# Order of background work in a two-layer attention kernel: queries before keys for one chunk, more background calls in steps with many row maxima, and a shorter lead of the maxima

## The reference, cut to what matters

```
layer 0:  x0, x1 = halves of x (1024 rows each)
          x0 += gate * attention(ln(x0) modulated)      # each half on itself
          x1 += gate * attention(ln(x1) modulated)
          x0 attends to keys/values of x1, and x1 to those of x0 (cross)
          x += gate * mlp(ln(x) modulated)              # gelu, 256 -> 1024 -> 256
layer 1:  x = ln(x + attention(x, x, x, masked))        # 512 valid keys
          x = ln(x + attention(x, context, context))    # 1601 keys
          x = ln(x + mlp(x))                            # relu
```

## Time and profile before

| | |
|---|---|
| runs, us | 2201.14, 2204.52, 2205.17 (median 2204.52) |
| profiled execution, its own time | 2205.17 us |
| its span | 2203.3 us |
| TensorE busy | 1991.3 us, 90% of the span |
| VectorE busy | 1539.9 us, 70% |
| ScalarE busy | 1293.3 us, 59% |
| GpSimd busy | 565.4 us, 26% |
| mean granted share of TensorE's clock | 0.945 |

### The profile page before, as it was taken

One profiled execution on the slowest core, in us unless ns is written; L12 is line 12 of the kernel. 1 busy time (PEld: TensorE's weight loads), 2 busy tenths in 40 slices (PEclk: granted clock), 3 DMA queues, 4 the chain that ended last, 5 costly groups with the idle time before them and its releaser, 6 DMA issues. The chain is left out here.

```text
span 2203.3 us, 33892 instructions
## 1 busy us (share of the span) xinstructions
PE 1991.3 (90%) x12890; PEld 769.1 (35%) x12890; DVE 1539.9 (70%) x2841; ACT 1293.3 (59%) x2406; POOL 565.4 (26%) x537
## 2 busy tenths in 40 slices
PE   5898998998979899998999988999899999999976
PEld 3333222332323343533533432332253334334315
DVE  5777797797857658476376557896847996896704
ACT  1155585566746676764775653678335874684670
POOL 1135775751123211032022332210204001102100
PEclk8699999999989999999999997999799999999988
DMA  6733423422243202035024422200211020000000
GB/s 155 154 86 87 128 83 83 106 59 49 64 89 77 62 6 55 20 73 121 4 62 102 92 61 73 59 21 14 42 40 37 4 50 3 14 17 4 13 16 12
DMA packets 97338, 126.67 MB, mean 57 GB/s; under 512 B 25325, under 2 KB 82014, under 8 KB 92046
## 3 DMA queue, kind: packets, MB, share of 16 engines
q1 hardware_dynamic: 94862, 123.89, 23.7%
q10 hardware_dynamic: 2304, 0.53, 0.1%
HBM read 89.95 MB, written 24.74 MB: 52 GB/s over the span
## 5 line engine op out<-in xcount | busy, mean ns | idle before, releaser
L1691 ACT ACTIVATE PT<-ps 128x512 f32<-128x512 f32 (+1 forms) x2112 | 1109.0, 601 | 700.1 <-PE ps L1476 696.2
L1774 DVE TENSOR_REDUCE mx<-ps 128x1 f32<-128x512 f32 x2048 | 1283.7, 681 | 263.8 <-PE ps L1497 261.1
L1497 PE MATMUL ps<-KS,QS 49*128 49x512 bf16 x2048 | 744.2, 399 | 124.1 <-DVE mx L1774 63.5
L1476 PE MATMUL ps<-QS,KS 51*128 51x512 bf16 (+3 forms) x4224 | 816.7, 388 | 11.3 <-DMA QS<-mr 11.0
L1523 PE MATMUL ps<-PT,Vt 128*32 128x512 f32 (+1 forms) x4224 | 584.3, 626 | 0.0
L1497 PEld LDWEIGHTS ps<-KS,QS 49*128 49x128 bf16 x2048 | 188.0, 95 | 734.1 <-DVE mx L1774 454.8
L1476 PEld LDWEIGHTS ps<-QS,KS 51*128 51x128 bf16 (+3 forms) x4224 | 235.8, 96 | 238.6 <-ACT PT L1691 64.8
L2008 POOL CAST nm<-nm 128x16 bf16<-128x16 f32 x64 | 12.7, 198 | 513.2 <-DVE nm L1787 513.1
L1523 PEld LDWEIGHTS ps<-PT,Vt 128*32 128x32 f32 (+1 forms) x4224 | 84.2, 109 | 150.2 <-issue 147.5
L1618 PE MATMUL ps<-XT,big 128*128 128x256 f32 x512 | 126.7, 398 | 3.5 <-ACT big L1747 2.6
L1630 PE MATMUL ps<-big 128*128 128x256 f32 x512 | 114.8, 382 | 1.6 <-DVE big L1909 1.6
(11 more groups left out here) (110 smaller groups left out, 1100.8 us busy)
## 6 DMA issues: line engine op xcount, KB each, us to landing
scr<-S SPq DMA_DIRECT2D x27, 768.0 KB, 3.7
big<-in_mask_1x1xSxS_ik SPq DMA_DIRECT2D x16, 1024.0 KB, 5.2
QS<-scr SPq DMA_DIRECT2D x32, 384.0 KB, 9.6
KS<-scr SPq DMA_DIRECT2D x24, 384.0 KB, 8.7
QS<-scr SPq DMA_DIRECT2D x32, 256.0 KB, 6.1
ON<-Oe SPq DMA_DIRECT2D x256, 32.0 KB, 1.9
OD<-scr_r SPq DMA_DIRECT2D x32, 256.0 KB
KS<-scr SPq DMA_DIRECT2D x24, 256.0 KB, 4.8
```

The source lines that it names most:

```text
L1476: z = eng.matmul(ps[0:w, it.bank[1 - j], :], KS[lo:hi, part, pr, col:col + w], QS[lo:hi, part, u.qs, pr, :], start=part == 0, stop=part == ...
L1497: return eng.matmul(mbank(it)[:, 0:w], QS[lo:lo + MR, 0, u.qs, pr, 128 * it.tq:128 * it.tq + 128], KS[lo:lo + MR, 0, pr, it.lo:it.hi], sta ...
L1691: eng.activation(PT[0:w, it.pt * 4 + 2 * it.pp + 1 - k, :], ps[0:w, it.bank[k], :], ACT.Exp, scale=0.25).then_inc(S["exp_done"], 1)
L1774: eng.tensor_reduce(out=mx[:, u.b, c, it.i:it.i + 1], in_=mbank(it)[:, 0:it.hi - it.lo], axis=AX.X, op=ALU.max).then_inc(S["max_done"], 1)
```

## The change

Three edits: `LEAD` goes from 9 to 7; in a step with more than two tasks of maxima, `bg_step` is called after each task but the last; and in `kv_l0` the query projection comes ahead of the key projection and V.

```diff
-LEAD = 9
+LEAD = 7
@@
                     for task in now_[:-1]:
                         for g in task:
                             g()
+                        if len(now_) > 2:
+                            bg_step()
@@
-            return (ln_mod(c, g) + k_steps(512 * c, 512, f"k_in{c}", over, 4 * g) + v_steps(4 * c, 512, c, over)
-                    + (q_steps(c, slot, 4 * g) if slot is not None else []))
+            return (ln_mod(c, g) + (q_steps(c, slot, 4 * g) if slot is not None else [])
+                    + k_steps(512 * c, 512, f"k_in{c}", over, 4 * g) + v_steps(4 * c, 512, c, over))
```

## The result

The changed kernel took 2220.97 us (median of 4 runs, 2220.02 to 2223.06), the kernel before 2204.23 us (2201.14 to 2205.17). The ratio is 1.0072, 95% interval 1.0052 to 1.0092: slower by 0.7%, where I had forecast 2190 us and faster. The profiled execution has a span of 2218.1 us against 2203.3.

What follows compares the result with a forecast made beforehand. TensorE and VectorE were taken as both full in plain steps. Queries -11.1, calls -5.0 and -1.0, LEAD +2.5 sum to -14.6 us from 2205.17, so 2190.6, forecast as 2190 us; 8 in 10 for 2178 to 2206.

Steps and rivals of the forecast that it cites:

- an MLP at half clock: Second heavy stretch: two thirds of the moved MLP pieces run at half clock, +18 us, about 2213 us; chance 0.12.
- The third rival: Gains and losses cancel: queries edit brings only 7, stretches nothing, maxima rows cost 11, less 1.5; about 2207 us; chance 0.15.
- What bounds the kernel: Plain steps: TensorE and VectorE both full; time won only at TensorE waits, half clock, or where only one is full.
- my 3.1: Chunk 3's projection: TensorE stands still while the second eviction into `xn` waits for GpSimd, +3.1 us.
- -2.3 us of half clock: Chunk 3, 643.10 to 648.40: the half-clock stretch behind the queries' old wait goes, -2.3 us.
- -5.0 us for the second stretch: Second heavy stretch: extra calls bring the MLP inside; overlap, pace and clock gains less VectorE work sum to -5.0 us.
- the last ten slots at the plain pace: Second heavy stretch: last ten slots, behind dense TensorE work, run at 1.25 rather than 1.4 us a pair, -1.5 us.
- I had -1 us: First heavy stretch: its only background comes four steps earlier, nothing else is eligible; -1 us, between -4 and +3.
- I take +4, a third of the way: LEAD edit: later delivery of maxima rows costs +4 us in crowded places, from a range of 0 to 12.
- waits appeared in the 1601-key passes: Sign against the prediction: `QS<-mr` waits there; it expected 11 to 20 us in all, all before 900 us.
- the +12: LEAD edit: upper end of the late-delivery cost by the DMA rule alone, putting the kernel at about 2199 us.
- The -1.5 us at the end: Kernel's end: 2 of 35 steps without maxima get them, filling TensorE's room; -1.5 us, between -3 and 0.

## Why the prediction was wrong, point by point

**The number.** I forecast 2190 us and had 8 in 10 for 2178 to 2206; it is 2221, 30 us more. By the runs, some 22 of these are LEAD (24 us beside the other edits, I had +2.5), 7 the queries ahead of keys (-4.2, I had -11.1), and the calls little more than 1. Slower had a chance of 0.12, but by another mechanism, an MLP at half clock, which did not come. The third rival had the right mechanism, with 11 us for the maxima rows; its sum is 2207.7.

**What bounds the kernel.** Held. The work at full clock was the same before and after (1898.7 and 1898.6 us), and time moved only with waits and clock.

**Queries ahead of keys: right in kind, too large.** The wait near 643 is gone and the one for `xn` is there, 3.87 us against my 3.1 (ScalarE was idle for 5.88 before its eviction, where I had 3 to 4). Timeline of the kernel after:

```profile
635.42 2.12 POOL L2038 TENSOR_TENSOR S<-xn,S 128x1024 bf16<-128x1024 f32 x1
637.57 0.37 SPq L1288 DMA_DIRECT2D scr<-S  x1
637.64 0.69 ACT L1731 ACTIVATE xn<-ps,colb 128x512 f32<-128x512 f32 x1 [5.88 <-POOL S L2038]
...
638.38 3.78 PE L1584 MATMUL ps<-XT,wA 128*128 128x512 f32 x4 [3.87 <-ACT xn L1731]
```

I had priced the new wait at full clock. The four matmuls behind it took 3.78 us where the same work took 1.98: a half-clock stretch comes with this wait as it had come with the old one, 6.2 us behind it against the 5.3 of the earlier trace rows.

```profile
638.38:644.57 6.19, 6.19 (x18) 1.65 (x18) 2.04 (x3) 2.01 (x4) 1.42 (x2) 0.50 0.76 210
```

So the term "-2.3 us of half clock" did not hold. The edit brought 6.7 us in the profile and 4.2 by its ratio, not 11.1.

**Extra calls: right in sign.** I had -5.0 us for the second stretch, with bounds of 19 both ways. The traces show -8.6 and -5.1, the ratio of the run with the calls alone -4.6 for the whole kernel. The MLP ran inside, at 0.38 us for output pieces, so the rival with the MLP at half clock fell. Windows of the kernel after, the stretch and what follows (the two together answer to the third and fourth of the earlier trace rows):

```profile
1577.00:1625.00 48.00, 42.69 (x199) 24.88 (x200) 26.50 (x49) 9.85 (x20) 7.05 (x5) 0.86 0.08 13
1625.00:1662.00 37.00, 33.52 (x186) 12.64 (x189) 27.97 (x55) 14.55 (x28) 7.58 (x7) 0.77 0.06 19
```

The whole stretch is 69 us long (1577 to 1646; I had about 65). The second of these windows still holds the end of the MLP, whose last matmul is over at 1631.3. Cut there, the clock shows what each part did: 1.00 with the MLP's pieces between, 0.58 behind them, where pairs alone are left.

```profile
1593.50:1631.30 37.80, 34.52 (x176) 24.20 (x174) 15.02 (x28) 6.51 (x14) 1.27 (x1) 1.00 0.00 1
1631.30:1651.50 20.20, 16.72 (x71) 4.19 (x70) 17.92 (x38) 5.95 (x11) 7.58 (x7) 0.58 0.07 26
```

So the -1.5 us that I gave for "the last ten slots at the plain pace" is doubtful. In the first stretch (units 42 to 45) I had -1 us; the kernel after gained 0.8 there, the calls alone lost 2.4.

**LEAD: this is the step that failed.** "I take +4, a third of the way, since the crowd is issued at the same steps as before", with 0 to 12 as bounds and +2.5 for the whole edit. LEAD 7 measured +12 us alone and 24 beside the other edits. The term was mis-sized, and the traces show three things that it left out. First, I took the delay of a delivery as bounded by its old crowd, at most 2.5 us more; but issued later it fell behind query reads and a mask load that it had been ahead of. The waits for the maxima rows rose by 16.5 us. Second, such a wait brings half clock, and I had counted that for the queries' wait but not here. Behind the kernel after's six longest waits for these rows (2.8 to 6.7 us) the granted clock was 0.50 to 0.62 over the next 5 us (one of them lay in a half-clock stretch already); in the first pass half clock cost 8.5 us more than before. Third, I looked at the delivery alone. The two GpSimd operations before it have a queue of their own. Timeline near 1900 in the kernel after: the last reduction of the maximum starts at 1899.81, its split comes after two layer-norm products, at 1904.72, and the transpose waits 2.4 us for it. In the kernel before, 1887.09 and 1888.58, it was ahead of them.

```profile
1899.81 0.22 DVE L1789 TENSOR_REDUCE nm<-mx 128x16 f32<-128x64 f32 x1
1899.98 2.37 POOL L2067 TENSOR_TENSOR x<-x,G 128x1024 f32<-128x1024 f32 x1 [2.30 <-DVE x L1893]
1902.43 2.34 POOL L2070 TENSOR_TENSOR x<-x,G 128x1024 f32<-128x1024 f32 x1
1904.72 0.20 POOL L2010 CAST nm<-nm 128x16 bf16<-128x16 f32 x1
```

I had written that the prediction would be wrong if waits appeared in the 1601-key passes. Waits did appear there (5.2 us in two, where the kernel before had none, and 4.2 us lost between units 61 and 62), for this queue and not for `QS<-mr`. The rule of the Trainium skill that I had set against the edit, "DMA: Bandwidth & Descriptors" on taking turns between queues, pointed the right way; the +12 that I put beside it is what LEAD 7 costs alone, and half of what it costs beside the other edits.

**LEAD: what it was to win.** The -1.5 us at the end did not show: from unit 63 to the end the kernel after is 0.4 us faster.

**What stays open.** Why LEAD 7 costs twice as much beside the two edits as alone; some 5 us of the idle time that LEAD 11 removes; why the rows' first packet starts so late in a crowd; and how much of the run to run difference of LEAD 7 (2213 to 2228 us) is which load meets which delivery. That a different place for the mask loads with GpSimd's work kept even would help at LEAD 9 was not tried.

## What to carry to other kernels

A small transfer that a later step needs has no fixed latency: here 0.8 us in a quiet place, 7.2 behind 1.5 MB of other reads, and 10.8 with a 1 MB load on top. When its issue is moved, look at what was issued just *after* it in the old trace, not only at what it waited for. The slack of such a delivery was cheap to lengthen here (two steps, 2.5 us, gave 0.9 to 1.0%, and two more gave nothing) and dear to cut, since a miss can cost half clock too; and before one shortens a lead, the longer one is worth a run.

## What the runs showed of the hardware

The granted clock went to 0.50 after waits of some 4 us in a stretch that was otherwise full: after the 3.87 us wait near 638 the next four projection matmuls ran at 0.94 us each instead of 0.50, and the clock stayed there for 6.2 us of full work, which costs 3.1 us. Price a new TensorE wait with this tail, here nearly as much again as the wait. Shorter waits went both ways in the kernel after: behind one of 2.24 us ending at 1177.5 the clock was 0.50, behind one of 2.40 us ending at 1905.4 it was 1.00.

A delivery of 2 x 4 KB on ScalarE's queue landed between 0.8 and 12.9 us after its issue in these traces, late where SyncE had large transfers in flight.
